# Attention with 7 of 8 key tiles transposed by DMA instead of 6, and a part of the constants loaded later

## The reference

```python
# layer 0
h = group_norm(x, norm_w, norm_b)
qkv = jnp.einsum('bchw,dc->bdhw', h, qkv_w) + qkv_b[None, :, None, None]
q, k, v = jnp.split(qkv.reshape(B, 3 * C, N), 3, axis=1)
attn = jax.nn.softmax(jnp.einsum('bcn,bcm->bnm', q, k) * scale, axis=-1)
out = jnp.einsum('bnm,bcm->bcn', attn, v).reshape(B, C, H, W)
x = x + jnp.einsum('bchw,dc->bdhw', out, proj_w) + proj_b[None, :, None, None]
# layer 1
out = relu(batchnorm(conv2d(x, w1), g1, b1))
offsets = conv2d(out, w_off) + b_off[None, :, None, None]
x = relu(batchnorm(deform_conv(out, offsets, w2), g2, b2) + x)
```

## Time and profile before

| | |
|---|---|
| median of 3 runs | 2494.78 us (2494.53 to 2497.68) |
| the profiled execution | 2493.83 us |
| its span, first to last instruction | 2491.7 us |
| granted TensorE clock, mean | 0.970 |
| PE, DVE, ACT, POOL busy | 2315.7, 1855.8, 1795.1, 1310.9 us |
| DMA transposes of the attention | 512, issued from 49.5 to 1589.1 us |

### The profile page before, as it was taken

The page is one execution under the profiler, slowest core; times in us unless marked ns, Lnnn a source line. Parts: engine busy times, 40 slices in busy tenths (PEclk is TensorE's granted clock), DMA queues, the critical chain, the costliest instruction groups (busy, mean ns, idle before and its releaser), DMA issues.

```text
span 2491.7 us, 73903 instructions
## 1 busy us (share of the span) xinstructions
PE 2315.7 (93%) x27053; PEld 1877.2 (75%) x27053; DVE 1855.8 (74%) x3901; ACT 1795.1 (72%) x2963; POOL 1310.9 (53%) x1067
## 2 busy tenths in 40 slices
PE   5999999999999999999999999799877999899992
PEld 3777777777777777777777777588447999899992
DVE  6778777778877777877777777587666877777875
ACT  5778888878888888888888888532556766666754
POOL 4557545555545555544555555663116665556650
PEclk9999999999999999999999999899898999999996
DMA  3878887778787877877777777771224433333336
GB/s 108 166 144 147 141 162 140 147 149 146 145 159 133 150 145 145 150 129 129 149 147 146 148 146 148 192 235 59 66 71 133 124 113 113 111 111 117 115 95 270
DMA packets 917462, 345.25 MB, mean 139 GB/s; under 512 B 844256, under 2 KB 904160, under 8 KB 909024
## 3 DMA queue, kind: packets, MB, share of 16 engines
q1 hardware_dynamic: 917216, 341.87, 63.6%
HBM read 98.76 MB, written 41.68 MB: 56 GB/s over the span
## 4 chain that ended last, share of the span: by engine, by line
PE 75%; issue 9%; POOL 7%; DVE 4%; DMA 3%; ACT 1%; SPq 1%; POOLq 0%; DVEq 0%; ACTq 0%
PE psum L1041 14%; PE psum L1042 14%; PE psum L1043 14%; POOL probs_split L363 7%; PE psum L1080 7%; PE psum L1082 7%; PE psum L1081 7%; PE psum L1222 5%; PE psum L1066 3%; DMA probsT_dma<-probs_split 1%; PE psum L1195 1%; DMA final<-x_scratch 1%; DVE padded_hi L946 0%; PE psum L1120 0%; PE psum L1203 0%
## 5 line engine op out<-in xcount | busy, mean ns | idle before, releaser
L363 POOL TENSOR_TENSOR probs_split<-probs,probs_split 128x768 f16<-128x768 f32 x512 | 841.8, 1644 | 697.0 <-ACT probs_split L512 696.8
L711 DVE TENSOR_REDUCE neg_max<-psum 128x1 f32<-128x1024 f32 x512 | 626.6, 1224 | 333.0 <-PE psum L1043 332.8
L509 ACT ACTIVATE probs<-psum,exp_bias 128x1024 f32<-128x1024 f32 x512 | 570.2, 1114 | 220.2 <-DVE exp_bias L713 215.6
L1080 PE MATMUL psum<-vT_hi,probsT_dma 128*128 128x129 f16 x3072 | 549.6, 221 | 4.1 <-DMA probsT_dma<-probs_split 4.1
L1082 PE MATMUL psum<-vT_hi,probsT_dma 128*128 128x129 f16 x3072 | 549.5, 219 | 0.0
L1081 PE MATMUL psum<-vT_lo,probsT_dma 128*128 128x128 f16 x3072 | 549.4, 218 | 0.0
L512 ACT ACTIVATE probs_split<-probs 128x768 f16<-128x768 f32 x512 | 431.7, 843 | 22.8 <-ACT probs L509 1.0
L455 POOL TENSOR_TENSOR interp<-row_hats,col_hats 128x360 f32<-128x360 f32 x384 | 294.4, 795 | 219.6 <-PE psum L1222 214.7
L1041 PE MATMUL psum<-k_hi,q_hi 128*128 128x512 f16 x1024 | 387.8, 379 | 3.9 <-DVE q_lo L827 2.4
L1042 PE MATMUL psum<-k_lo,q_hi 128*128 128x512 f16 x1024 | 388.1, 379 | 0.0
L1043 PE MATMUL psum<-k_hi,q_lo 128*128 128x512 f16 x1024 | 388.1, 379 | 0.0
(11 more groups left out here) (181 smaller groups left out, 5532.1 us busy)
## 6 DMA issues: line engine op xcount, KB each, us to landing
xt_windows<-xt_scratch SPq DMA_DIRECT2D x192, 320.0 KB
xt_scratch<-zeros_f SPq DMA_DIRECT2D x28, 576.0 KB, 4.4
probsT_dma<-probs_split SPq DMA_TRANSPOSE x512, 3.7
x_residual<-x SPq DMA_DIRECT2D x128, 64.0 KB, 2.6
x_scratch<-x_out SPq DMA_DIRECT2D x128, 64.0 KB, 2.4
x_rows<-x_scratch SPq DMA_DIRECT2D x32, 256.0 KB, 3.4
xt_scratch<-xt_stage SPq DMA_DIRECT2D x128, 64.0 KB
final<-x_scratch SPq DMA_DIRECT2D x16, 512.0 KB, 10.7
```

Of the source, the lines that this page charges most:

```text
L363: po.tensor_tensor(PH[:, j, 1, :], P[:, j, 0:DW], PH[:, j, 0, :], ALU.subtract).then_inc(s["pl"], 1)
L509: act.activation(P[:, j, :], sc, ACT.Exp, bias=NB[:, par, j:j + 1]).then_inc(s["exp"], 1)
L711: ve.tensor_reduce(NM[:, par, j:j + 1], sc, AX.X, ALU.max, negate=True).then_inc(s["mx"], 1)
L1080: pe.matmul(dst, th, Vh[:, p, v, 0:129], start=n == 0, stop=False)
```

## The change

The number of key tiles that go by DMA becomes a list with one entry per chunk, all four of them 7. So each DMA transpose carries 2 x 7 tiles, ACT's and POOL's halves are 896 columns wide, PE transposes one tile of a unit and the evictions are 128 columns wide. The four buffers of each kind become tensors of their own, one for each chunk.

Of the constants, only the first K_LO columns are loaded at the start. The others go to a new tensor `late_constants`, loaded on SP's queue behind the zero rows of layer 1 and ahead of the wait for them; it lies in memory that the attention used. The operation that makes `offset_high` moves behind the first norm's last step, with a wait for that load ahead of it.

```diff
-DT = 6
-DW = 128 * DT
+DT = (7, 7, 7, 7)
...
-        CN = sb_in(ctx, "constants", [128, K_ALL], F32)
+        CN = sb_in(ctx, "constants", [128, K_LO], F32)
...
-        PH = sb_in(l0, "probs_split", [128, CPT, 2, DW], F16)
-        PDT = sb_in(l0, "probsT_dma", [128, CPT, 2, DT, 128], F16)
-        PTh = sb_in(l0, "probsT_hi", [128, CPT, KT - DT, 128], F16)
-        PTl = sb_in(l0, "probsT_lo", [128, CPT, KT - DT, 128], F16)
+        PH = [sb_in(l0, f"probs_split{j}", [128, 2, 128 * d], F16) for j, d in enumerate(DT)]
+        PDT = [sb_in(l0, f"probsT_dma{j}", [128, 2, d, 128], F16) for j, d in enumerate(DT)]
+        PTh = [sb_in(l0, f"probsT_hi{j}", [128, KT - d, 128], F16) for j, d in enumerate(DT)]
+        PTl = [sb_in(l0, f"probsT_lo{j}", [128, KT - d, 128], F16) for j, d in enumerate(DT)]
...
+        CL = sb_in(l1, "late_constants", [128, K_ALL - K_LO], F32)
...
-            sp.dma_start(CN[:, :], consts).then_inc(s_k, 16)
+            sp.dma_start(CN[:, :], consts[:, 0:K_LO]).then_inc(s_k, 16)
...
-                        sp.dma_start_transpose(PDT[:, j, :, :, :].rearrange("p e m q -> p (e m) q"),
-                                               PH[:, j, :, :].rearrange("p e k -> p (e k)")).then_inc(s_tr[j], 16)
+                        sp.dma_start_transpose(PDT[j][:, :, :, :].rearrange("p e m q -> p (e m) q"),
+                                               PH[j][:, :, :].rearrange("p e k -> p (e k)")).then_inc(s_tr[j], 16)
...
+            sp.dma_start(CL[:, :], consts[:, K_LO:K_ALL]).then_inc(s_kl, 16)
             sp.wait_ge(s_zf, 16 * 28)
...
-                    po.tensor_tensor(PH[:, j, 1, :], P[:, j, 0:DW], PH[:, j, 0, :], ALU.subtract).then_inc(s["pl"], 1)
+                    po.tensor_tensor(PH[j][:, 1, :], P[:, j, 0:128 * DT[j]], PH[j][:, 0, :], ALU.subtract).then_inc(s["pl"], 1)
...
-                    act.activation(PTh[:, (j + 2) % 4, :, :].rearrange("p m q -> p (m q)"), PS[:, 4 + j % 2, 0:CH - DW],
+                    k = (j + 2) % 4
+                    act.activation(PTh[k][:, :, :].rearrange("p m q -> p (m q)"), PS[:, 4 + j % 2, 0:CH - 128 * DT[k]],
                                    ACT.Copy).then_inc(s["hi"], 1)
...
-                    act.activation(PH[:, j, 0, :], P[:, j, 0:DW], ACT.Copy).then_inc(s["ph"], 1)
+                    act.activation(PH[j][:, 0, :], P[:, j, 0:128 * DT[j]], ACT.Copy).then_inc(s["ph"], 1)
...
-            link(ve.tensor_scalar(HIGH[:, :, :], low, float(HH + 1), None, ALU.add))
             after(ve, "bs", B * NCH)
             norm(L1_VAR1, 10, vec(V_G1), vec(V_B1), 1)
             assert lstep[0] == L1_AB1
+            ve.wait_ge(s_kl, 16)
+            link(ve.tensor_scalar(HIGH[:, :, :], low, float(HH + 1), None, ALU.add))
...
-                for m in range(KT - DT):
-                    last = pe.transpose(PS[:, bank, 128 * m:128 * m + 128], P[:, j, DW + 128 * m:DW + 128 * m + 128], ident)
+                for m in range(DT[j], KT):
+                    at = 128 * (m - DT[j])
+                    last = pe.transpose(PS[:, bank, at:at + 128], P[:, j, 128 * m:128 * m + 128], ident)
...
-                    m = (n + DT) % KT
+                    m = (n + DT[j]) % KT
```

More of the change, by code:

```diff
@@ L195, in build @@
         s_k = sem("constants_loaded")
+        s_kl = sem("late_constants_loaded")
         s_zf = sem("zero_rows_stored")
@@ L662, in half_image @@
                                 sampled(q - 1, (g + 1) % 2, i)
-                act.activation(SM[:, 32:34], CN[:, bass.ds((n + first_pass) * 2 + K_SH, 2)], ACT.Copy).then_inc(s["sh"], 1)
+                act.activation(SM[:, 32:34], CL[:, bass.ds((n + first_pass) * 2 + (K_SH - K_LO), 2)], ACT.Copy).then_inc(s["sh"], 1)
                 after(act, "sh", n + 1)
@@ L698, in _ @@
             boff = WF[:, W_BOFF:W_BOFF + NOFF][:, None, :].to_broadcast([128, GPI, NOFF])
-            low = CN[:, K_LO:K_SH].rearrange("p (q k) -> p q k", q=GPI)
+            low = CL[:, 0:K_SH - K_LO].rearrange("p (q k) -> p q k", q=GPI)
             ve.wait_ge(s_wh, 1)
@@ L722, in unit @@
                     k = (j + 2) % 4
-                    ve.tensor_tensor(PTl[:, k, :, :].rearrange("p m q -> p (m q)"), PS[:, 4 + j % 2, 0:CH - DW],
-                                     PTh[:, k, :, :].rearrange("p m q -> p (m q)"), ALU.subtract).then_inc(s["lo"], 1)
+                    ve.tensor_tensor(PTl[k][:, :, :].rearrange("p m q -> p (m q)"), PS[:, 4 + j % 2, 0:CH - 128 * DT[k]],
+                                     PTh[k][:, :, :].rearrange("p m q -> p (m q)"), ALU.subtract).then_inc(s["lo"], 1)
                 if late4:
@@ L967, in _ @@
             l1(ve.tensor_scalar(SM[0:1, 30:31], SM[0:1, 29:30], REACH, None, ALU.is_gt))
-            l1(ve.scalar_tensor_tensor(CNT[0:1, :], CN[0:1, K_CA:K_CB], SM[0:1, 30:31], CN[0:1, K_CB:K_ALL], ALU.mult, ALU.add))
+            l1(ve.scalar_tensor_tensor(CNT[0:1, :], CL[0:1, K_CA - K_LO:K_CB - K_LO], SM[0:1, 30:31], CL[0:1, K_CB - K_LO:K_ALL - K_LO], ALU.mult, ALU.add))
             assert lstep[0] == L1_FLAG
@@ L1073, in values @@
                 for n in range(KT):
-                    m = (n + DT) % KT
+                    m = (n + DT[j]) % KT
                     if m == 0:
                         pe.wait_ge(s_tr[j], T_ * 16 + (16 + OPEN))
-                    th, tl = (PTh[:, j, m - DT, :], PTl[:, j, m - DT, :]) if m >= DT else (PDT[:, j, 0, m, :], PDT[:, j, 1, m, :])
+                    th, tl = (PTh[j][:, m - DT[j], :], PTl[j][:, m - DT[j], :]) if m >= DT[j] else (PDT[j][:, 0, m, :], PDT[j][:, 1, m, :])
                     v = 8 * j + m
```

## The result

The changed kernel took 2437.32 us (median of 4 runs, 2433.26 to 2445.52) beside 2494.66 us for the kernel before on the same chip (4 runs): ratio 0.9773 [0.9746, 0.9800], 57.3 us less. The forecast was 47.7 us less, 2447 us, with a range of 2440 to 2462: the direction and the main cause were right, the gain was 10 us larger, with 10.4 us from a stage for which the forecast had no term, and the median lies 2.7 us outside the range. The profiled execution of after took 2438.34 us (span 2436.4), 55.5 us under the profiled one of before.

The account below looks back on a forecast made before the run. The prediction took TensorE to bound the kernel. Its terms summed to -47.7 us, taking the profiled 2493.8 us to 2446.1; with the median of runs 1.0 above, 2447 us, range 2440 to 2462 (8 in 10).

Parts of the forecast that it names:

- TensorE, -55.3: Attention: TensorE loses one 0.108 us transpose in each of 512 units, 55.3 us less while it stays the bound.
- ScalarE, no change of load: Attention copies: one widens to 896 columns, +0.12 us, the other narrows to 128, -0.12 us; load unchanged.
- POOL, +0.27: Attention: POOL's L363 step takes 1.91 us for 896 columns, +0.27, hidden but delaying the transfer behind it.
- The transposes: Attention DMA queue: 14 tiles need 2.25 us of a 2.76 us unit, not the bound; landing about 0.3 us later.
- Rivals A and B: Attention: A, landing becomes the bound, about 2473 us, chance 0.12; B, DMA queue becomes the bound, about 2535, chance 0.05.
- Slack 3.1 to 1.7 us: Plain attention unit: slack between transpose landing and first matmul reading it shrinks by 1.4 us to 1.7, so cover holds.
- Three waits behind image loads, +4.2: Attention, three places behind next-image loads where slack is already gone: each wait grows 1.4 us, +4.2 in all.
- the end, +0.8: Last attention units, only latency left: copy 0.12, POOL 0.27, landing 0.3 and a tile more behind the wait, +0.8 us.
- POOL at 190 to 233 us, +1.5: Stretch with convolution-weight steps: POOL becomes the bound and falls behind; 1.5 us counted, between 0 and 3.
- Stragglers, +1.0: Attention: a few single landings above 5 us overrun the reduced slack, +1 us, between 0 and 4.
- Constants: Start gains nothing, late load costs nothing (0.5 us if uncovered), offset_high moved behind the norm gives -0.4 us.

Follow-up runs that it names:

- e5: Changed kernel with 1216 already-met waits (608 instructions) put into PE's program between the attention and layer 1; 2503.13 us, ratio 1.0044.
- e12: Changed kernel with 192 already-met waits (96 instructions) put into PE's program between the attention and layer 1; 2453.67 us, ratio 0.9832.
- e8: Changed kernel with two unused 128 KB loads more per query tile, behind the transposes of chunks 1 and 2; 2488.36 us, ratio 0.9978.
- e9: Changed kernel with the loads of images 2 and 3 in eight pieces each, the load of image 1 whole; 2432.18 us, ratio 0.9752.
- e10: Changed kernel with query tiles 12 to 19 of images 1 and 2 as a loop instead of written out; 2437.09 us, ratio 0.9764.
- e3: Kernel before with only the late constants load and the moved offset_high operation, six tiles by DMA; 2493.90 us, ratio 0.9991.
- e1: Kernel before run again without edit, for a second profile; 2495.58 us, ratio 0.9998.
- e2: Changed kernel run again without edit, for a second profile; 2437.31 us, ratio 0.9764.

## Why the prediction was right in kind and short in size

**The step that failed** is the one that isn't there. The sum was made over the attention and the norm; the deformable stage had no term, on the ground that nothing in it was edited. The edit took 608 instructions out of PE's written program ahead of the loop, and the pauses of the loop behind it went from 30.1 to 21.4 us; e5 gives them back by putting 608 instructions in that do nothing. With the 1.7 us that I put down to the clock after the pauses that is -10.4 us. The profile of before showed the pauses (PE held by nothing for 30.1 us, six times), and I read past them, because they were not to change. The profile of before doesn't tell the sign of such an effect: e12, with 96 instructions more than after, takes 14.7 us more in this stage than after, and 4.3 more than before.

The other steps, in their order:

1. *TensorE, -55.3.* Right: units of 2.76 us, 0.108 less, and a plain query tile went from 11.62 to 11.19 us.
2. *ScalarE, no change of load.* Right: L515 takes 950 ns (0.96 forecast), and ACT is busy 168.06 of 200 us (at most 168 forecast).
3. *POOL, +0.27.* Right: 1889 ns (1.91 forecast) against 1644, +0.25.
4. *The transposes.* The landing is right, 4.0 us. The drain is not what I took it for: I had 2.25 us for 14 tiles. Behind the first image load SP's queue in after shows (start, duration of the issue, line; then the time to landing of the transposes issued at 60.32 and at 76.41, the last of the four)

```profile
60.32 5.57 SPq L265 DMA_TRANSPOSE probsT_dma<-probs_split  x1
65.94 0.63 SPq L274 DMA_DIRECT2D x_residual<-x  x1
66.67 11.30 SPq L265 DMA_TRANSPOSE probsT_dma<-probs_split  x4
...
DMA to landing us min/median/max: 10.4/10.4/10.4
...
DMA to landing us min/median/max: 4.1/4.1/4.1
```

so landings at 70.7 and 80.5, four transposes in 9.8 us, 2.44 us each, 0.174 us a tile instead of 0.16. But neither quotient is a rate of the queue. The last of the four was issued 3.7 us behind the one ahead of it and landed after an ordinary 4.1 us, as the last one of before landed after an ordinary 3.8, so the queue had caught up by then, and 2.44 and 1.9 us are upper bounds. The spare of the queue is at least 2.76 - 2.44 = 0.3 us a unit, before residual loads and stores are counted; what it is, no run shows, and e8 shows that there is some. Rivals A and B did not occur. The Trainium skill, page "VectorE: DVE Perf Modes", gives TensorE 390 ns and the crossbar 1309 ns for a 128x128 transpose in bfloat16 (section "The three transpose paths") and advises TensorE where PSUM will do (section "Rules for kernel authors"). Here the seventh tile on the crossbar made the attention 44 us shorter, since a tile costs at most 0.174 us there in a queue of its own and 0.108 us on the engine that sets the time.
5. *Slack 3.1 to 1.7 us.* Right: over all units, from the landing to the first matmul that reads it, the median went from 3.1 to 1.6. In a plain unit of after the exponential starts at 902.21 and the first matmul that reads the transposed tiles at 911.88, 9.67 us later; it was 10.54.
6. *Three waits behind image loads, +4.2, and the end, +0.8.* Right in place, too small for this execution: the tiles at the three loads are 2.94, 1.3 and 2.44 us longer than the rule of -0.43 a tile, 6.7 in all. PE in after at the first:

```profile
70.73 0.23 PE L1085 MATMUL psum<-vT_hi,probsT_dma 128*128 128x129 f16 x1 [2.67 <-DMA probsT_dma<-probs_split]
...
70.00:76.00 6.00, 5.27 (x46) 3.65 (x47) 2.16 (x3) 1.74 (x3) 1.89 (x1) 0.72 1.18 176
```

The wait is 2.67 us, and behind it the granted clock is 0.72 over 6 us: (1 - 0.72) x 6 / 0.5 = 3.4 us of them at the lower of the two levels. That price, the clock after a wait, wasn't in the term. It isn't paid in every execution: over the five of the same attention the three tiles lose 2.9 us (e5, where the clock didn't fall at these places) to 7.0, so 4.2 lies inside their range, and only four of the five are above it. e9 gets 3.8 us back with the later two loads in pieces; after lost 3.74 there. The end cost +1.1 where +0.8 less 0.4 for the last four units was forecast.
7. *POOL at 190 to 233 us, +1.5.* Right in mechanism: POOL is busy 43.00 of 43.00 us there (38.83 in the earlier trace rows). Tiles 12 to 17 lost 2.5 us. PE's wait there is 1.1 us in two places, within the 1 to 3 that I had said.
8. *Stragglers, +1.0.* What remains of the loss in the attention, 54.9 - 43.95 - 6.7 - 2.5 = 1.8 us. e10 shows what the late landings are: transposes that run beside a fetch of instructions.
9. *Constants.* The start gained nothing (unit 0 starts at 44.2 us in both), the late load was hidden, and `offset_high` stands behind the norm. DVE in after:

```profile
1700.15 0.16 DVE L914 TENSOR_TENSOR small<-weights_f,small 128x1 f32<-128x1 f32 x1
1700.35 0.46 DVE L920 TENSOR_SCALAR offset_high<-late_constants 128x576 f32<-128x576 f32 x1
1701.25 0.43 DVE L950 CAST padded_hi<-h_rows 128x512 f16<-128x512 f32 x1 [0.44 <-ACT h_rows L608]
```

It takes 0.46 us, and the wait for ACT behind it is 0.44 instead of 0.94. The stage of the first convolution is 1.1 us shorter; e3 has 0.4 of it with the constants alone, and the rest isn't explained.

The sum as it should have been: -55.3 + 6.7 + 1.5 (the end) + 2.5 + 1.8 - 0.4 - 10.4 = -53.6, against -55.3 measured; the 1.7 left lie in the first convolution, its norm and the last stage. My steps overstated the attention's gain by 4.4 us (with its end: 47.3 forecast, 42.9 measured) and left out 10.4: with the deformable stage as it was, the kernel would have come out at 2437.3 + 10.4 = 2447.7 us. That this is nearly the forecast's 2447 is luck in part: the 4.4 us are offset by the 1.7 us of the other stages and by 2 us of the medians, since I put the median 1.0 us above the profiled execution and after's lies 1.0 below it.

## What to carry to other kernels

When work goes from the engine that sets the time to one with room, most of the gain comes through as long as the slack of the plain unit holds; the losses sit where that slack was gone before (bulk loads, a second user of the helping engine, the end), and they grow faster than the moved work: 1.1 us of 27.4 for the first half of it, 9.8 for the second (6.4 to 11.2 by the scatter of after's attention). And where a kernel has long loops behind the edited code, look in them for pauses that no wait explains, compare them one by one in both traces, and leave some 10 us (0.4% here) on either side of the forecast for the edit's effect on where they lie; a gain of that kind can be taken away again by the next edit.

## What the runs showed of the hardware that I had not expected

- TensorE pauses 2.6 to 7.3 us at each return of a loop whose passes take 70 us. The pause is the same to some tenths of a us when the kernel is run again, and goes with the place of the loop in the engine's program. Fetches of 16 KB of instructions lie in these pauses. The DMA queues in the pause at 2012.5 to 2017.5 us of before, and then in the one at 2039 to 2042 us of after:

```profile
q8 instruction: 2, 0.03, 4.6%
```

```profile
q8 instruction: 1, 0.02, 2.6%
```

  Two in the longer, one in the shorter. It is so in all of them: each of the 24 pauses of before, e1, e5 and e12 (4.2 to 7.3 us) has two fetches that begin in it or at most 0.4 us ahead of it, and each of the 24 of after, e2, e8 and e10 (2.7 to 5.1 us) has one. That the engine waits for them is an inference from this, and no run took a fetch away there.
- A fetch of 16 KB takes one DMA engine 0.97 us at the median in the attention of after (0.88 to 1.75), and a transpose that runs beside it lands later, 4.7 against 4.0 us at the median.
- After a wait of PE of 2.7 to 3.3 us in an otherwise busy stretch the granted clock was at the lower level for 3.4 us in some executions and not in others of the same attention code; a query tile with the fall is about 2 us longer.
- A wait that is already met isn't free on TensorE's program: 608 instructions of two waits each held it 66.0 us.
- A DMA share of 0.96 isn't a full queue: 256 more loads of 128 KB cost 0.164 us each.
